# Flamingo block with mixture of experts: routing rebuilt, row maxima in blocks, later slots

## The reference

```python
x = x + tanh(g_xattn) * attention(layernorm(x), ctx)      # 8 x 256 tokens of 128, 16 heads of 8
x = x + tanh(g_ffn) * experts(layernorm(x))               # 2048 tokens, 8 experts, top 2

# attention: keys are 64 context rows and the 256 tokens, causal over the tokens; out @ Wout + bout
# experts:
capacity = int(T / E * 1.25)                              # 320
gate_logits = xt @ Wg + bg
top_v, top_i = top_k(gate_logits, 2)
expert_label = one_hot(top_i, E).sum(axis=1)
seq = cumsum(expert_label, axis=0) * expert_label
valid = (seq > 0) & (seq <= capacity)                     # who comes too late for an expert is dropped
flat_idx = where(valid, expert * capacity + seq - 1, E * capacity)
disp = rows placed at flat_idx, per expert [320, 128]
out = (silu(disp @ W1) * (disp @ W2)) @ W3                # H = 512
y = sum over the two choices of softmax(top_v) * out at the token's place
```

## Time and profile before

| | us |
|---|---|
| runs | 308.89, 305.91, 308.52 |
| median | 308.52 |
| profiled execution | 304.91 |
| its span, first to last instruction | 303.1 |

### The profile page before, as it was taken

The page is one execution under the profiler, slowest core; times in us unless marked ns, Lnnn a source line. Parts: engine busy times, 40 slices in busy tenths (PEclk is TensorE's granted clock), DMA queues, the critical chain, the costliest instruction groups (busy, mean ns, idle before and its releaser), DMA issues.

```text
span 303.1 us, 6031 instructions
## 1 busy us (share of the span) xinstructions
PE 238.4 (79%) x2179; PEld 140.7 (46%) x2179; DVE 174.1 (57%) x532; ACT 132.0 (44%) x294; POOL 152.9 (50%) x213
## 2 busy tenths in 40 slices
PE   1767784888988777897997789885979999999800
PEld 0555322355554444454554444342346666666600
DVE  6479691758889899877758963544102333333400
ACT  6256501757665566655546666312013333333200
POOL 3699820445352763817417548355500555655661
PEclk9999966979999999977569999997889999999985
DMA  7131365464533226561010001001054455553220
GB/s 199 38 84 47 67 118 85 76 119 99 118 57 58 54 51 94 106 190 43 16 37 13 16 18 40 0 16 43 4 122 125 118 120 125 126 127 57 22 22 5
DMA packets 28764, 21.79 MB, mean 72 GB/s; under 512 B 4105, under 2 KB 26051, under 8 KB 28736
## 3 DMA queue, kind: packets, MB, share of 16 engines
q1 hardware_dynamic: 21632, 15.74, 22.7%
q0 software_dynamic: 4608, 4.16, 7.9%
q10 hardware_dynamic: 2496, 1.52, 2.5%
HBM read 9.27 MB, written 5.82 MB: 50 GB/s over the span
## 4 chain that ended last, share of the span: by engine, by line
PE 34%; DVE 14%; issue 14%; DMA 13%; POOL 13%; ACT 5%; ACTq 2%; POOLq 1%; SPq 1%; another core or an unknown queue 0%; DVEq 0%
PE PS L1120 11%; DMA out<-kst 7%; PE PS L1100 6%; POOL out L633 5%; DMA qst<-mrow 4%; DVE rows L881 2%; PE PS L1083 2%; DVE mxb L836 2%; DVE mxb L835 2%; PE PS L1058 2%; PE PS L1170 2%; ACT pt L696 2%; POOL slots L598 2%; PE PS L1274 1%; PE PS L1276 1%
## 5 line engine op out<-in xcount | busy, mean ns | idle before, releaser
L696 ACT ACTIVATE pt<-PS 128x512 f32<-128x512 f32 x128 | 72.0, 596 | 41.5 <-PE PS L1100 38.8
L1100 PE MATMUL PS<-qst,kst 49*128 49x256 bf16 (+2 forms) x384 | 51.6, 250 | 8.1 <-DMA qst<-mrow 6.8
L633 POOL DMA_INDIRECT out<-kst x24 | 36.4, 1518 | 41.9 <-DVE kst L1004 19.0
L1120 PE MATMUL PS<-pt,vp 128*32 128x256 f32 (+2 forms) x768 | 47.8, 343 | 8.6 <-ACT mrow L689 7.5
L835 DVE TENSOR_REDUCE mxb<-PS 128x2 bf16<-128x384 f32 x64 | 35.5, 555 | 29.7 <-PE PS L1083 27.3
L836 DVE TENSOR_REDUCE mxb<-PS 128x2 bf16<-128x640 f32 x64 | 52.3, 817 | 0.0
L1100 PEld LDWEIGHTS PS<-qst,kst 49*128 49x128 bf16 x384 | 30.5, 100 | 31.5 <-issue 14.7
L991 DVE TENSOR_TENSOR kst<-PS,kst 128x320 f32<-128x320 f32 x32 | 15.7, 492 | 49.8 <-ACT kst L765 49.8
L598 POOL DMA_INDIRECT slots<-rows,dest x32 | 32.2, 1007 | 19.6 <-DVE dest L962 12.8
L577 POOL TENSOR_SCALAR_AFFINE_SELECT pt<-pt 128x512 f32<-128x512 f32 x32 | 21.5, 672 | 38.6 <-ACT pt L696 38.5
L1078 PE MATMUL PS<-kst,qst 48*128 48x320 bf16 x128 | 33.4, 335 | 0.0
(11 more groups left out here) (129 smaller groups left out, 382.5 us busy)
## 6 DMA issues: line engine op xcount, KB each, us to landing
kp<-in_w SPq DMA_DIRECT2D x24, 256.0 KB, 2.9
kst<-kp SPq DMA_DIRECT2D x30, 80.0 KB
qst<-qp SPq DMA_DIRECT2D x36, 64.0 KB
slots<-blank POOLq DMA_DIRECT2D x4, 325.0 KB, 4.5
kst<-slots SPq DMA_DIRECT2D x8, 130.0 KB, 2.4
out<-xs SPq DMA_DIRECT2D x4, 256.0 KB
kst<-kp SPq DMA_DIRECT2D x14, 40.0 KB
xs<-in_x SPq DMA_DIRECT2D x2, 256.0 KB, 4.6
```

Of the source, the lines that this page charges most:

```text
L633: nc.gpsimd.indirect_dma_start(out=tokens, out_offset=bass.IndirectOffsetOnAxis(ap=ex[0:n, e, s, D:D + 1].bitcast(u32), axis=0), in_=yr[0: ...
L696: nc.scalar.activation(pt[:, U % 2, h, :], PS[:, 4 + h % 2, :], ACT.Exp, scale=SCALE).then_inc(exp_done, 1)
L1100: c = nc.tensor.matmul(PS[:, 4 + par, c0:c1], keys_of(r, gp)[:, g0 + p, i, k0:k0 + 128], queries_of(r, gp)[:, g0 + p, i, q0:N], start=True ...
L1120: c = nc.tensor.matmul(O[VW * j:VW * j + VW, q0:N], vblock(b, chunk, g0 + j, par), pt[:, V % 2, 2 * j + par, c0:c1], start=(chunk == 0 and ...
```

## The change

- maxima: one reduce over 16 blocks of 64 keys (2 heads x 8) into mx8; after the fourth pair two small reduces (unit_maxima) give mxb. maxima_t waits for these, and is written before the second half of the turned scores of its block.
- normalize: one operation of 128 x 128 instead of two; the layout of att changes, and wout is loaded in four pieces to suit it.
- tokens_out: from VectorE to ScalarE, x * rstd + shift with shift = -mean * rstd from GpSimd, both copies of the row at once. The ScalarE copy of the second goes.
- The exponential is taken from the two largest logits (second_exponentials, two instructions), the weights are computed by GpSimd (weights).
- The one-hot is compared as integers and stays apart for both choices; positions adds the counts so far by a matmul with lastrow (one row of ones) in fp32, from base, the copy of the last positions, which starts at e*2048 - 1. So the own position is already the destination; each expert has 2048 places (dram tensor places, 16384 rows), and nothing is dropped. The experts load the first 320 of each, and those alone are cleared, in eight DMAs instead of four.
- Slots: the steps from turn_values on stand three (turn_values), two (until x1) and two to four slots later, and the last two batches are no longer hurried up to their one-hots.

```diff
-        SLOTS = E * CAP
+        SLOTS = E * T
-        AT_OT = 2 * SL + 1
-        AT_INV = 2 * SL + 3
-        AT_NORM = 2 * SL + 4
-        AT_ATTT = 2 * SL + 6
+        AT_OT = 2 * SL + 4
+        AT_INV = 2 * SL + 5
+        AT_NORM = 2 * SL + 6
+        AT_ATTT = 2 * SL + 8
...
+                pool.wait_ge(rstd_ready, len(GROUPS) + 2 * b + 1)
+                for t in range(2):
+                    c = nc.gpsimd.tensor_scalar(shift2[:, b % 2, t:t + 1], mv2[:, b % 2, t, 0:1],
+                                                rstd2[:, b % 2, t:t + 1], -1.0, ALU.mult, ALU.mult)
+                c.then_inc(rstd_ready, 1)
+
+            def weights(b):
+                pool.wait_ge(e01_done, b + 1)
+                nc.gpsimd.tensor_scalar(s01[:, :], e01[:, :], 1.0, 1.0, ALU.mult, ALU.add).then_inc(wts_done, 1)
+                pool.wait_ge(wts_done, S_WTS * b + 1)
+                nc.gpsimd.tensor_tensor(rows[:, b, 0, :, D + 1], s01[:, :], invert2[:, :], ALU.pow).then_inc(wts_done, 1)
+                pool.wait_ge(wts_done, S_WTS * b + 2)
+                nc.gpsimd.tensor_tensor(rows[:, b, 1, :, D + 1], e01[:, :], rows[:, b, 0, :, D + 1], ALU.mult
+                                        ).then_inc(wts_done, 1)
...
-                nc.scalar.copy(rows[:, b, 1, :, 0:D], rows[:, b, 0, :, 0:D]).then_inc(row1_done, 1)
+            def tokens_out(b):
+                act.wait_ge(rstd_ready, len(GROUPS) + 2 * b + 2)
+                for i in range(2):
+                    xv = xs[:, 2 * b + i, :]
+                    c = nc.scalar.activation(rows[:, b, :, i, 0:D],
+                                             bass.AP(tensor=xv.tensor, offset=xv.offset, ap=[xv.ap[0], [0, TOPK], [1, D]]),
+                                             ACT.Identity, scale=rstd2[:, b % 2, i:i + 1],
+                                             bias=shift2[:, b % 2, i:i + 1])
+                c.then_inc(h2_ready, 1)
...
-                nc.vector.tensor_reduce(mxb[:, U % 2, 0, :, p], PS[:, a:a + 2, 0:192], axis=AX.X, op=ALU.max)
-                nc.vector.tensor_reduce(mxb[:, U % 2, 1, :, p], PS[:, a:a + 2, 192:512], axis=AX.X,
-                                        op=ALU.max).then_inc(max_done, 1)
+                nc.vector.tensor_reduce(mx8[:, :, p, :], PS[:, a:a + 2, :].rearrange("p q (c k) -> p q c k", k=64),
+                                        axis=AX.X, op=ALU.max).then_inc(max_done, 1)
+            def unit_maxima(U):
+                dve.wait_ge(max_done, UP * (U + 1))
+                if U >= 2:
+                    dve.wait_ge(mT_ready, U - 1)
+                nc.vector.tensor_reduce(mxb[:, U % 2, 0, :, :], mx8[:, :, :, 0:3], axis=AX.X, op=ALU.max)
+                nc.vector.tensor_reduce(mxb[:, U % 2, 1, :, :], mx8[:, :, :, 3:8], axis=AX.X, op=ALU.max
+                                        ).then_inc(unit_max, 1)
...
+                    nc.vector.tensor_copy(base[:, (b + 1) % 2, :], pv[:, 1, :]).then_inc(base_ready, 1)
+                if step == 1:
+                    dve.wait_ge(picked, b + 1)
...
+                    nc.vector.tensor_reduce(dest[:, b % 2, :], ohp[:, :, :], axis=AX.X, op=ALU.max
+                                            ).then_inc(dest_ready, 1)
...
+                for t in range(2):
+                    nc.tensor.matmul(pos[:, t, :], lastrow[:, :], before, start=True, stop=False)
+                    for i in range(2 * t):
+                        nc.tensor.matmul(pos[:, t, :], ones[:, :], oh[:, i, :], start=False, stop=False)
+                    nc.tensor.matmul(pos[:, t, :], tri[:, :], oh[:, 2 * t, :], start=False, stop=False)
+                    c = nc.tensor.matmul(pos[:, t, :], tri[:, :], oh[:, 2 * t + 1, :], start=False, stop=True)
+                c.then_inc(pos_ready, 1)
```

261 lines of the change are left out of this document (119 added, 142 removed).

## The result

The changed kernel takes 297.34 us in the median of four runs (295.48 to 298.60). The kernel before, on the same chip, takes 308.19 (305.91 to 308.89). The ratio is 0.9655, with a 95% interval of 0.9582 to 0.9728: faster by 10.9 us. In a second measurement, beside seven runs of the kernel before, it took 299.37 us (ratio 0.9768, 0.9679 to 0.9857). That ratio leaves out runs that took over 1.5% more than the fastest of their kernel, as three of the seven of the kernel before did (their median is 308.22). The prediction was 299.0, so the total came out.

The account below looks back on a forecast made before the run. VectorE was taken to hold up TensorE in the attention batches. Batch terms of -10.6 us and tail +0.9 gave -9.7, from 304.91 to 295.2; shifted by 3.6 to the median, 299.0, range 292 to 307.

Parts of the forecast that it names:

- The structure of a batch: Attention batch at full clock: TensorE 14.3 + 0.6 for positions + 1.0 wait = 15.9 us, 1.97 less than 17.87.
- The wait at positions: TensorE, before positions: a new wait of 1.0 us per batch for x1 of the next batch.
- mrow's wait: TensorE, before the values' matmuls: the 0.55 us wait for the ScalarE copy mrow vanishes, 7.0 us over the stage before.
- The clock: Attention stage: full clock kept for full-clock batches, 0.63 of full kept from 138.1 to 161 us, where 1.0 is gained.
- VectorE holds TensorE up: Attention batches: TensorE stands idle 3.1 to 4.0 us because of VectorE, whose load falls 2.4 to about 13.4 us.
- Its reading of d: VectorE operation d: 0.490 us in the mean, 0.14 once, where no GpSimd select ran beside it.
- The new operations: Per batch: fused reduce 1.21 us, unit maxima 0.8 in all, ScalarE activations 0.41 to 0.60 each, GpSimd 14.0 afterwards.
- rival B: GpSimd becomes the bound: its new operations cost 0.5 each, it needs 16.9 us per batch, total 304.1; chance 0.15.
- The tail: After 200.8 us, routing up to the last landed send: +0.9 us; sign: last send 0 to 1 us later after last values.
- A: The clock recovers: denser TensorE keeps 2.4 GHz, the slow stretch takes 15.9 instead of 21.9, total 293.0; chance 0.17.
- C: The gain vanishes: the chain passes to VectorE's maxima and exponentials, a batch gives 0.4 us, total 307.8; chance 0.12.
- D: Slower by the new wait at positions: x1 comes 3 us late instead of 1, batch 18.5, total 312.4; chance 0.08.

Follow-up runs that it names:

- the one with old slots: The changed kernel with the slots from turn_values to 1/std as in the kernel before, only the work changed: 301.47 us.

## Why the prediction came out

**The structure of a batch: near.** 15.9 us was predicted; the batches take 15.9 to 16.0 with their whole clock loss taken off, and 16.53 in the one measured at full clock. The wait at positions is 1.07 where 1.0 was worked out, and mrow's wait is gone. Two terms were off, with opposite signs. TensorE is busy 14.53 us in that batch where 14.9 was worked out: positions takes 0.66 us until the next block where it took 0.21, 0.45 more and not 0.6. And it is idle 2.0 us, not 1.0: the sum had no term for exponentials, for which TensorE waits twice 0.37 in that batch and 4.4 us in 13 places over the stage. (The 14.3 taken for the batch before is that of two of the three; the third has 14.82.)

**The clock: wrong, and it is the step that failed.** The prediction took the full clock for the batches that had it, and 0.63 for 138 to 161. It named the new wait, priced it at its length, and treated the clock only as a rival that might recover. In fact a fall follows the wait and the small matmuls behind it in nearly every batch, and filling the wait takes four of five such falls away. In numbers between the 4th and the 16th mrow copy: 5.5 batches times 1.84 us of structure would be 10.1 us, the prediction's terms there sum to 9.4, measured was 109.82 - 104.43 = 5.4. The loss to the clock was the same 10 us in both kernels, but before it cost less: the long stretch lengthened its batch from 17.9 to 22.95, by 5.1 us for some 17 us at the low clock, 0.3 per us, as TensorE had 3 to 4 us of idle time in a batch to give. After, it costs 0.5 per us. A denser engine pays the whole fall.

**The total: right, in part by chance.** The other 4 us came from places where nothing was predicted. The 4th mrow copy comes 2.7 us earlier in the first profile and 0.6 in the second, so most of that is not the change. From the 16th copy to the last values' copy 1.4 was gained (1.2 predicted; 0.1 in the second profile). From the last landing to the end both profiles after are 1.3 shorter; before has a clock of 0.66 between 224.9 and 229.9 us there, and the first scatter-add comes 18.0 instead of 16.5 us after the landing. Sum in the first profile: -2.7 - 5.4 - 1.4 + 1.4 - 1.3 = -9.4, predicted -9.7. (The shift of 3.6 us to the median makes 298.8 of 295.2; 299.0 is that, rounded up.)

**VectorE holds TensorE up: wrong.** The load fell as predicted, from between 15.3 and 16.3 us to between 13.1 and 13.6, but putting 3.3 us of load back lengthens a batch by 0.2 to 0.4. What TensorE waited for were places in the order. Its reading of d was off too: d took 0.14 to 0.15 us three times of seven, not once, and one of these (0.15 at 126.27) ran beside the selects. The four that took 0.51 to 1.06 all did. The terms of the batch were built from those places, which is why the number came out though the sentence was wrong.

**The new operations: near.** The fused reduce (the page's groups), then one of the unit maxima and the rows on ScalarE (by line: duration in ns, least, median and most):

```profile
L880 DVE TENSOR_REDUCE mx<-PS 128x16 bf16<-128x1024 f32 x64 | 76.9, 1210 | 27.5 <-PE PS L1097 26.7
...
L887 DVE TENSOR_REDUCE mxb<-mx x16: 178/178/179, 39.9 to 167.3; 128x8 bf16<-128x24 bf16 x16
...
L751 ACT ACTIVATE rows<-xs,shift,rstd x16: 584/589/600, 81.8 to 199.5; 128x256 f32<-128x256 f32 x16
```

The reduce takes the predicted 1.21. The activation takes 0.589, at the upper end of the 0.41 to 0.60 that was given; by the Trainium skill (ScalarE: Activation LUTs, What ACT_TABLE_LOAD costs) the estimate was 585 ns, and the trace agrees. GpSimd's busy time per batch is 11.6 to 11.8, less than the 14.0 worked out, which counted the pauses between sends as well. It waits 12 us for exponentials in three batches; rival B was never near.

**The tail: +0.9 predicted, with 0 to 1 as the sign, +1.4 and +0.5 measured** (19.15 before; 20.51 and 19.66 after). veps was said to stay in place, but in the first profile it starts 2.57 us behind x1 instead of 2.13, behind weights and two sends; in the second it does stay in place (2.16). The landing takes 2.30 instead of 2.09, 0.2 where 0.3 was taken:

```profile
209.53 2.30 DMA places<-rows,dest
```

**The rivals.** B, C and D did not happen as mechanisms. A, the clock recovers, happened only where the wait was filled or removed: its 293.0 is close to what the two kernels with x1 early or positions late take, 292.6 and 293.1, but by other steps (batches of 15.4, and falls left), so that agreement is of numbers alone. D had the right place and the wrong reason: its wait never reached 3 us, and its harm came through the clock.

## What to carry to other kernels

Price a new wait on TensorE by more than its length: look at what stands around it, and if small matmuls follow, ask for the clock in the rows. Compare batches at equal clock before asking which engine binds, and test the bound by putting work back. Take off a clock loss at its full length only where the engine has no idle time left. Once TensorE is dense, a fall of the clock costs half its length, so a few filler matmuls in the last waits can be worth more than the work that was saved: here 297 to 299 us went to 285 by three slot numbers and two filler matmuls per batch, though part of that stands outside the stretch where the filler acts.

## What the runs showed of the hardware

- The clock fell to half behind a wait of 0.37 us, when eight matmuls of 8 columns (two of them fp32) followed: four times in four like batches, 2.2 to 2.3 us behind the start of positions. With 0.43 us of filler ahead of them it did not fall there at all. Filler with a wait of 1.07 us left one of five.
- What part the small matmuls have is not shown. The kernel before waited up to 1.07 us (at 102.89) between 83 and 119 us without a fall; on the other hand falls stand behind waits of 0.78 to 0.89 for an exponential, far from positions (103.1 and 107.9 in the two kernels with filler). No run kept the wait and left the small matmuls out, and whether the fp32 ones matter more than the bf16 ones was not tried.
- In the stage falls lasted 3.4 or 6.8 us in most cases, and about 17 in the long stretches of the kernel before and of the one with old slots.
- With its waits filled the kernel before repeats within 0.12 us in four runs; without, seven runs on the same chip spread over 9.3. What looks like noise of the chip can be the kernel's own clock.
- A single-source reduce of 256 columns takes 0.409 us from SBUF with one result per partition. It ran eight times per batch beside everything else for 0.2 to 0.4 us of batch.
- One fp32 VectorE operation of 128 x 128 on SBUF with two pointers took 0.33 to 0.35 us in most cases with no GpSimd select beside it, and 0.57 to 0.78 beside one.
